# The maxima over eight key tiles of an attention: two reductions from SBUF, or two maxima in place in PSUM and one reduction from there

## The reference

```python
qh = (layernorm(x) @ wq + bq)   # split into 16 heads of 32
kh, vh = ctx @ wk + bk, ctx @ wv + bv
attn = einsum('bhqd,bhkd->bhqk', qh, kh) / sqrt(32)
score = softmax(attn, axis=-1)                  # over 2048 keys
out = einsum('bhqk,bhkd->bhqd', score, vh) @ wo + bo
x = x + out
```

## Time and profile before

| | us |
|---|---|
| median of 3 runs | 3758.9 (3753.5 to 3764.3) |
| profiled execution, its own time | 3759.5 |
| its span, from the first to the last instruction | 3757.7 |
| mean granted TensorE clock | 0.942 |

### The profile page before, as it was taken

How to read it: one execution, slowest core, us unless ns; L and a number is a source line. 1 busy time by engine, 2 the same in 40 slices (tenths; PEclk the granted TensorE clock), 3 DMA queues, 4 the chain that set the end, 5 groups by cost and what they waited for, 6 DMA issues and landing times.

```text
span 3757.7 us, 76838 instructions
## 1 busy us (share of the span) xinstructions
PE 3377.8 (90%) x30330; PEld 2738.4 (73%) x30330; DVE 2700.1 (72%) x3275; ACT 1666.2 (44%) x2082; POOL 2130.4 (57%) x1520
## 2 busy tenths in 40 slices
PE   9888898888889889888888988887499999999999
PEld 7677776677677767767767767775378888888888
DVE  4666766766676676676667667667587768879997
ACT  3555555555555555555555555555212332231111
POOL 2566776776777667667767667765455500013332
PEclk9999999999999999999999999998799999999999
DMA  4111111111111111111111111111212243330000
GB/s 152 43 49 39 50 53 45 45 46 54 45 45 53 43 48 51 48 44 46 55 38 52 53 43 48 46 54 62 77 60 93 95 139 101 111 108 18 23 22 17
DMA packets 232245, 217.33 MB, mean 58 GB/s; under 512 B 17377, under 2 KB 181089, under 8 KB 230753
## 3 DMA queue, kind: packets, MB, share of 16 engines
q1 hardware_dynamic: 231904, 212.62, 18.4%
HBM read 174.14 MB, written 38.40 MB: 57 GB/s over the span
## 4 chain that ended last, share of the span: by engine, by line
PE 58%; DVE 23%; issue 16%; POOL 1%; ACT 1%; DMA 0%; DVEq 0%; SPq 0%; POOLq 0%; ACTq 0%
PE a_bank L103 41%; DVE x_folds L1482 14%; PE a_bank L1643 6%; DVE x_s L1503 5%; PE a_bank L1627 4%; PE a_bank L1663 2%; PE a_bank L1670 1%; PE a_bank L854 1%; DVE x_acc L1517 0%; PE a_bank L1653 0%; PE a_bank L2584 0%; PE a_bank L865 0%; PE a_bank L929 0%; DVE x_acc L1513 0%; POOL x_pairs L1271 0%
## 5 line engine op out<-in xcount | busy, mean ns | idle before, releaser
L1482 DVE TENSOR_REDUCE x_folds<-x_s 128x256 f32<-128x2048 f32 x256 | 969.6, 3832 | 19.9 <-ACT x_s L1374 19.9
L103 PE MATMUL a_bank<-x_ctx,x_wk 128*128 128x512 f32 x3072 | 892.8, 438 | 0.0
L103 PE MATMUL a_bank<-x_wv,x_ctx 128*128 128x512 f32 x3072 | 800.8, 412 | 0.0
L103 PEld LDWEIGHTS a_bank<-x_ctx,x_wk 128*128 128x128 f32 x3072 | 618.4, 208 | 139.5
L103 PEld LDWEIGHTS a_bank<-x_wv,x_ctx 128*128 128x128 f32 x3072 | 609.3, 203 | 142.0 <-issue 15.3
L1268 POOL TENSOR_TENSOR x_pairs<-x_s 128x1024 f32<-128x1024 f32 x128 | 303.7, 2373 | 704.0 <-ACT x_s L1387 704.0
L1271 POOL TENSOR_TENSOR x_pairs<-x_pairs,x_s 128x1024 f32<-128x1024 f32 x256 | 613.3, 2396 | 20.1
L1503 DVE TENSOR_TENSOR x_s<-x_s,a_bank 128x1024 f32<-128x1024 f32 x512 | 610.2, 1213 | 7.7 <-ACT a_bank L1381 7.6
L1374 ACT ACTIVATE x_s<-a_bank 128x1024 f32<-128x1024 f32 x512 | 497.2, 1023 | 175.0 <-PE a_bank L1627 175.0
L1387 ACT ACTIVATE x_s<-x_s 128x2048 f32<-128x2048 f32 x256 | 489.0, 1910 | 11.4 <-DVE x_s L1503 10.7
L1393 ACT ACTIVATE x_shift_rows<-a_bank 32x128 f32<-32x128 f32 x128 | 34.2, 267 | 794.5 <-PE a_bank L1670 794.5
(11 more groups left out here) (199 smaller groups left out, 4697.7 us busy)
## 6 DMA issues: line engine op xcount, KB each, us to landing
x_tile_raw<-in_ctx SPq DMA_DIRECT2D x248, 256.0 KB, 3.8
x_staged<-shifts SPq DMA_DIRECT2D x128, 256.0 KB, 3.5
m_ff_src<-in_w_ff SPq DMA_DIRECT2D x44, 192.0 KB, 2.5
wq_ff<-m_ff_dst SPq DMA_DIRECT2D x44, 192.0 KB, 1.8
s_attT<-attT SPq DMA_DIRECT2D x16, 512.0 KB, 4.0
m_w_raw<-in_w SPq DMA_DIRECT2D x32, 256.0 KB, 3.0
f_w_in<-wq_ff SPq DMA_DIRECT2D x22, 256.0 KB, 3.3
q_x<-in_x SPq DMA_DIRECT2D x16, 256.0 KB, 4.0
```

The source lines that it names most:

```text
L103: mm = pe.matmul(out, lhs[a], rhs[b], start=first and n == 0, stop=last and n == 2)
L1482: dve.tensor_reduce(folds[:, cols(h, 2)], scores_of(s)[:, cols(h, 2)].rearrange("p j t s -> p j s t"), AX.X, ALU.max).then_inc(folded, 1)
```

## The change

`fold(s, h)` no longer reduces eight tiles from SBUF. When the second half of the scores of two heads has been copied to SBUF, it takes the elementwise maximum of that half, which still lies in PSUM, and of the first half's copy in SBUF, and writes it back in place in PSUM (128 x 1024 elements). A new `fold_tiles(s)` waits for both and reduces the four tiles left, for all four heads at once, from PSUM into `folds`: 128 x 2048 elements read with a step of one tile (512 bytes), 128 x 512 written. `folded` counts three per block instead of two. `folds` is 4 KB at offset 199 instead of 2 KB at 201, which covers the output bias's row; so SP loads the bias only after the last turn of the folds, and VectorE adds the first input after the last block's step instead of before it.

```diff
+    FOLDS = 3
...
-        folds = sc.at("x_folds", [P, HG, S], F32, 201)
+        folds = sc.at("x_folds", [P, HG, 2, S], F32, 199)
...
             late.load_weights(sp, 0)
-            late.load_output_bias(sp)
             late.load_tile(sp, FIRST)
...
             end_step(BLOCKS - 1)
+            sp.wait_ge(folds_turned, START + BLOCKS)
+            late.load_output_bias(sp)
             sp.wait_ge(table_made, START + BLOCKS)
-            sp.wait_ge(folds_turned, START + BLOCKS)
             late.load_first_rows(sp)
...
             def fold(s, h):
+
                 dve.wait_ge(kept, START + s.count(HG, 3 + h))
+                two = cols(h, 2)
+                here = bank[:, two].rearrange("p j (t s) -> p j t s", t=TPC)
+                dve.tensor_tensor(here, here, scores_of(s)[:, two, 0:TPC], ALU.max).then_inc(folded, 1)
+
+            def fold_tiles(s):
+                dve.wait_ge(folded, START + s.count(FOLDS, 2))
                 if s.back(1).exists():
                     dve.wait_ge(folds_turned, START + s.count())
-                dve.tensor_reduce(folds[:, cols(h, 2)], scores_of(s)[:, cols(h, 2)].rearrange("p j t s -> p j s t"),
+                dve.tensor_reduce(folds[:, :, 0], bank[:, 0:HG].rearrange("p j (t s) -> p j s t", t=TPC),
                                   AX.X, ALU.max).then_inc(folded, 1)
...
                     fold(s, 0)
                     fold(s, 1)
+                    fold_tiles(s)
...
             end_step(BLOCKS - 2)
+            end_step(BLOCKS - 1)
             late.add_input(dve, FIRST)
-            end_step(BLOCKS - 1)
...
-                pe.wait_ge(folded, START + s.count(2, 2))
+                pe.wait_ge(folded, START + s.count(FOLDS, FOLDS))
...
-                    mm = pe.transpose(bank[:, misc_bank(s), cols(j, S)], folds[:, j], id_t[:])
+                    mm = pe.transpose(bank[:, misc_bank(s), cols(j, S)], folds[:, j, 0], id_t[:])
```

## The result

The changed kernel took 3296.5 us (median of 4 runs, 3295.6 to 3297.1) against 3756.6 for the kernel before, a ratio of 0.877 with a 95% interval of 0.876 to 0.879. The forecast was 3347 us with a range from 3320 to 3490: the sign, the wait that goes and the price of every new operation came out as predicted, but the blocks became shorter than forecast. The profiled execution took 3295.6 us, its span is 3293.8.

The account below looks back on a forecast made before the run. Bound: a loop of TensorE's strips and VectorE's folds, TensorE waiting 2.4 us a block. 3759.5 - 409 (blocks) - 1.6 (first turn) - 2 (end) = 3347 us, chance 0.58; own range 3320 to 3375, with rivals up to 3490.

Parts of the forecast that it names:

- the sign: Whole kernel: faster by more than 0.3%, chance 0.90; no change 0.02; slower 0.08.
- the wait that goes: TensorE's wait for VectorE's reductions before the turn of the folds, 2.27 us in the block shown, would vanish.
- The removed and added operations: VectorE's folds: two maxima 2.35 us a pair, 0.04 us, one PSUM reduction 2.29 us; 4.68 us instead of 7.60.
- The half clock: TensorE's fall to 1.2 GHz after an idle stretch would go; rival that it stays or another wait grows: chance 0.12.
- The first rival: PSUM reduction: the step costs as in SBUF, 3.83 us, leaving a 0.9 us wait; 3460 us; chance 0.20 including 4.42 us.
- The distance of the turns: Steady attention blocks: turns of the folds 16.65 us apart instead of 19.95, a gain of 409 us over 124 intervals.
- the turn of the shifts is not late either: Behind the turn of the folds: VectorE's shift columns, 0.69 + 0.16 + 0.16 us, fit beside 1.5 us of TensorE's products.
- What is late next: At the turn of the folds: folds end 0.6 us early and may take up to 5.3 us before the wait returns.
- The end: End of the attention: 5.8 us gained on bare folds, 3.8 us lost to the later bias; net 2 us gained.
- The start: First turn of the folds: its own wait of 1.65 us would go, 1.6 us in the sum.
- dear rivals: Step as in SBUF, 3460 us (chance 0.20 with its dearest form, left out), and half clock staying, 3474 us (0.12).

Follow-up runs that it names:

- e2: The kernel before, its two reductions reading the same 2048 elements of SBUF each as neighbours instead of with a step of 512 bytes: 3282.5 us, ratio 0.875.
- e5: The changed kernel with one further reduction of all four heads from PSUM ahead of the one that counts (folds 2.2 us later): 3535.1 us, ratio 0.942.
- e4: The changed kernel with two further reductions (three heads, and 1024 elements of two heads) ahead of the one that counts, folds 2.8 us later: 3738.1 us, ratio 0.996.
- e5b: The changed kernel with one further reduction of one head from PSUM ahead of the one that counts (folds 0.6 us later): 3335.7 us, ratio 0.888.
- e3: The changed kernel with one further reduction of two heads from PSUM ahead of the one that counts (folds 1.1 us later): 3401.0 us, ratio 0.906.
- e1: The kernel before, its two reductions reading only the four key tiles of the second half from SBUF: 3284.0 us, ratio 0.875.
- e8: The kernel of e3 with shift_columns ahead of add_shift 2 on VectorE: 3387.8 us, ratio 0.902.
- e7: The kernel before with shift_columns ahead of add_shift 2 on VectorE: 3762.8 us, ratio 1.0016.
- e6: The changed kernel with the folds back in 2 KB at 201 and the output bias loaded early: 3287.5 us, ratio 0.875.
- e9: The changed kernel again, unedited, on the same chip as e6: 3292.6 us, ratio 0.877.
- e10: The kernel of e6 with add_input back ahead of the last block's step: 3290.9 us, ratio 0.876.

## Why the prediction was right and wrong

*The removed and added operations.* Right. Two maxima 1.22 us each (1.21 predicted), the reduction 2.29 us (2.29), the folds 4.68 us long, ending 0.5 us before TensorE turns them. The choice between 2.29 and 3.83 us was the heart of the forecast, and it was made on a judgement that no row backed: TensorE's rate into PSUM says nothing of how VectorE reads it with a step. That it came out was in part luck. e2 shows that in SBUF the step costs, and the changed kernel's row that in PSUM it doesn't. The Trainium skill (Advanced Engine Details and Errata, Memory Cachelines) states that SBUF is slower when each access goes to another cacheline, and the runs agree, with 3.83 against 2.28 us. For VectorE's reading of PSUM the trace shows no such price, with 2.29 us.

*The half clock.* Right: gone, 1.00 instead of 0.93. e5 and e4 bracket the idle stretch at which it comes back in this loop, 1.5 and 2.1 us a block. The first rival (a wait of 0.9 us with a full clock) would by these runs have kept it, as I said.

*The distance of the turns.* This is the step that failed, a term of the sum that was mis-sized: "16.70 us; with the other short intervals [...] I take 16.65", with 16.45 to 16.85 as its range. It is 16.20. The term was too long by 0.45 us, 124 x 0.45 = 56 us. I took a block with a wait and subtracted the idle time shown, as if everything else stayed. Two things go with the wait and are not in its row. The first is the turn of the shifts. Rows of VectorE and TensorE in the kernel before, which the prediction did not use, behind the turn of the folds at 1505.58:

```profile
1505.42 1.23 DVE L1503 TENSOR_TENSOR x_s<-x_s,a_bank 128x1024 f32<-128x1024 f32 x1
1506.55 0.70 DVE L1490 TENSOR_REDUCE x_shift_in<-a_bank 128x4 f32<-128x512 f32 x1
...
1507.70 0.33 PE L1670 MATMUL a_bank<-x_id,x_shift_in 128*128 128x128 f32 x1
```

2.12 us lie between the two turns, in the changed kernel 1.84. The prediction counted 1.0 us of shift columns beside 1.5 us of products and concluded that "the turn of the shifts is not late either". It left out that the columns start only behind add_shift 2 (L1503), 0.97 us after the turn; so they end when the products do, and the turn of the shifts comes 0.28 us later than it could. The second: the transposes now start 0.16 us before the products' end instead of behind a gap. Together 0.44 us. The other runs agree: distance less wait is 16.54 us in e5b, 16.61 in e3, 16.63 in e5, near my 16.65, and 16.2 only in the kernels whose folds end well before they are needed (the changed kernel, e1, e2). So 16.65 was the right value for a block that still waits, and no floor. The part of the shifts is shown by runs, in part: e8, and the short blocks of e7, give back 0.10 and 0.13 us a block with the columns moved ahead. The lost overlap is read from rows, and no run takes it away by itself.

*What is late next.* "The wait is gone with 0.6 us to spare" was right: 0.5 us in the rows above. But that "the folds may take up to 5.3 us" holds for the wait alone. The block grows earlier, through the shift columns: e5b, with 0.61 us more, waits at the turn of the folds for 0.01 us on the mean and has blocks 0.34 us longer. Drawn back in a line from e5b, e3 and e5, the growth would begin at 0.27 us, with folds of 5.0 us; no run lies in between.

*The end.* Predicted was a net gain of 2 us; from block 124's turn to the end it went from 1172.2 to 1170.6 us, 1.6. That is luck, for its parts were off and cancel. The bias landed in 3.3 us instead of 7.6, so that the product began 12.2 us after the last turn, not 16.3. And VectorE stood 5.45 us in front of a small copy in block 126, with no releaser, so that the last turn came 4.8 us later after block 124's than the prediction's steps give:

```profile
2153.46 0.29 DVE L1533 COPY x_acc<-a_bank 128x128 f32<-128x128 f32 x1 [5.45 <-issue]
```

e6, e9 and e10 have this too (5.9 to 6.3 us), the other kernels don't. What it is was not tested, but the trace has a hint. The queue that the page of the changed kernel calls "q14 instruction" moves a packet of 8 KB which ends 1.44 us before this copy starts, in each of the four traces, and in the other nine it moves none between 20 and 45 us after block 124's turn. So VectorE may have stood waiting for its next instructions; no run here takes the packet away.

*The start.* The first turn came 3.2 us later, not 1.65 earlier. I put that down to scatter and not to the change: over all kernels run it lies between 108.9 and 116.0 us, and between e9 and the first run of the same kernel it differs by about 1 us.

*The sum.* 3347 - 56 (distance) + 5 (start) + 0.4 (end) = 3296.4 us, against 3295.6 of the profiled execution. *The range* failed by its lower end: it took in dear rivals above and gave the floor of the block, which I had from subtractions of one kind, only 0.2 us downward. Over half of the evidence against it was a few rows away, at 1506.55 and 1507.70.

## What to carry to other kernels

When a wait is removed from a loop, take the new length from the work of the engine that stays, segment by segment, and not from the old length less the idle time shown: a second wait further on, and the overlap that it prevented, go with the first. A wait on TensorE can cost more than itself through the clock; here the last 0.6 us of a delay cost 1.6 us a block. Where VectorE reads with a step, look which memory it reads from: here the same step cost 1.5 us in SBUF and nothing in PSUM.

## What the runs showed of the hardware

VectorE's reduction of 2048 elements with a step of 512 bytes took 3.83 us from SBUF (3.58 us while the other engines idled) and 2.29 us from PSUM; with neighbouring elements it took 2.28 us from SBUF. VectorE's maximum of 1024 elements, in place in PSUM with one operand in SBUF, took 1.22 us, and its addition of the same size in place in SBUF 1.21. TensorE kept 2.4 GHz with an idle stretch of 1.5 us in every 18.1 us, and with 2.1 us in about 20 it fell to 1.2 GHz for a part of most blocks. A turn of the folds that nothing held up started 0.16 us before the shown end of the products ahead of it.
